# Layers 0, 2 and 3 of a diffusion transformer on one core: a block's outputs are turned back in the slot that turns a later block's maxima

## The reference, cut to what matters

```python
s = jnp.einsum('bqhd,bkhd->bhqk', q, k) * scale
a = jax.nn.softmax(s, axis=-1)
attn_out = jnp.einsum('bhqk,bkhd->bqhd', a, v).reshape(B, N, H)
x = x + gate_a[:, None] * (attn_out @ W_proj + b_proj)
```

## Time and profile before

| | |
|---|---|
| device time, three runs | 3444.96, 3454.8, 3452.23 us |
| the profiled execution: its own time | 3451.98 us |
| its span | 3450.2 us |
| mean granted TensorE clock | 0.95 of full |
| PE busy | 3162.4 us (92%) |
| DVE busy | 1824.0 us (53%) |
| ACT busy | 1467.0 us (43%) |
| POOL busy | 256.9 us (7%) |
| chain that ended last | PE 80%, DVE 10%, DMA 3%, ACT 3% |

### The profile page before, as it was taken

How to read it: one execution, slowest core, us unless ns; L and a number is a source line. 1 busy time by engine, 2 the same in 40 slices (tenths; PEclk the granted TensorE clock), 3 DMA queues, 4 the chain that set the end, 5 groups by cost and what they waited for, 6 DMA issues and landing times.

```text
span 3450.2 us, 52900 instructions
## 1 busy us (share of the span) xinstructions
PE 3162.4 (92%) x21156; PEld 1867.7 (54%) x21156; DVE 1824.0 (53%) x3812; ACT 1467.0 (43%) x2645; POOL 256.9 (7%) x278
## 2 busy tenths in 40 slices
PE   6899999999889999999389989999999999999987
PEld 3555665656566666666244445454454544554464
DVE  4876554563411322322278865757756577556433
ACT  0343535444322222221136645565455565565533
POOL 1100010001100000000100001001110101001010
PEclk9898999999898999999789999999999999999998
DMA  5200000002100000000321020001200000000000
GB/s 168 91 1 6 8 21 1 8 21 68 45 12 11 0 1 1 1 0 1 135 77 35 26 74 25 11 24 44 86 13 22 28 29 25 13 28 25 7 1 13
DMA packets 78713, 104.39 MB, mean 30 GB/s; under 512 B 18688, under 2 KB 52208, under 8 KB 78204
## 3 DMA queue, kind: packets, MB, share of 16 engines
q1 hardware_dynamic: 78468, 100.93, 8.9%
HBM read 72.05 MB, written 28.86 MB: 29 GB/s over the span
## 4 chain that ended last, share of the span: by engine, by line
PE 80%; DVE 10%; DMA 3%; ACT 3%; issue 2%; SPq 1%; POOL 1%; DVEq 0%; ACTq 0%; POOLq 0%
PE ps L978 73%; PE ps L1193 3%; DVE max_halves L1684 2%; DMA k_parts<-qk_parts 1%; PE ps L1320 1%; PE ps L1184 1%; DVE row_max_cross L1850 1%; DMA q_parts<-qk_parts 1%; PE ps L1172 1%; ACT big L2028 1%; ACT probs L2087 1%; DVE bn_stats L1720 1%; DMA q_blocks<-q_parts 1%; DVE xn_tok L1756 1%; SPq L879 1%
## 5 line engine op out<-in xcount | busy, mean ns | idle before, releaser
L2028 ACT ACTIVATE big<-ps 128x512 f32<-128x512 f32 x1280 | 693.7, 595 | 639.5 <-PE ps L978 638.6
L1684 DVE TENSOR_REDUCE max_halves<-ps 128x1 f32<-128x512 f32 x1024 | 650.4, 684 | 222.1 <-PE ps L978 219.4
L978 PE MATMUL ps<-k_groups,q_blocks 32*128 32x512 f32 x2048 | 451.6, 463 | 71.0 <-DVE qk_parts L1819 34.8
L978 PE MATMUL ps<-q_blocks,k_groups 32*128 32x512 f32 x2048 | 422.5, 466 | 3.3 <-DVE qk_parts L1819 2.0
L978 PE MATMUL ps<-big,probs 128*32 128x512 f32 (+2 forms) x3280 | 397.1, 531 | 5.0 <-ACT o_T L2003 3.8
L978 PE MATMUL ps<-weights_mlp,big 128*128 128x256 f32 (+1 forms) x1248 | 333.4, 419 | 2.5 <-ACT big L2099 2.5
L978 PEld LDWEIGHTS ps<-q_blocks,k_groups 32*128 32x128 f32 x2048 | 178.4, 185 | 286.1 <-issue 273.9
L978 PEld LDWEIGHTS ps<-weights_mlp,big 128*128 128x128 f32 x1248 | 233.7, 190 | 83.9 <-issue 58.0
L978 PEld LDWEIGHTS ps<-k_groups,q_blocks 32*128 32x128 f32 x2048 | 197.6, 189 | 120.9 <-DVE qk_parts L1819 39.0
L1726 DVE TENSOR_TENSOR x_tok<-ps,x_tok 128x512 f32<-128x512 f32 x112 | 77.3, 691 | 307.6 <-PE ps L978 307.4
L2087 ACT ACTIVATE probs<-ps 77x512 f32<-77x512 f32 x384 | 196.5, 592 | 96.8 <-PE ps L978 96.5
(11 more groups left out here) (233 smaller groups left out, 3913.6 us busy)
## 6 DMA issues: line engine op xcount, KB each, us to landing
q_blocks<-q_parts SPq DMA_DIRECT2D x64, 256.0 KB
q_parts<-qk_parts SPq DMA_DIRECT2D x48, 256.0 KB
k_parts<-qk_parts SPq DMA_DIRECT2D x32, 256.0 KB
k_groups<-k_parts SPq DMA_DIRECT2D x16, 512.0 KB
weights_mlp<-in_L_xcond_mlp_W SPq DMA_DIRECT2D x5, 1024.0 KB, 5.4
weights_mlp<-in_L_xcond_W_mlp SPq DMA_DIRECT2D x5, 1024.0 KB, 5.6
x_tok<-in_x SPq DMA_DIRECT2D x4, 1024.0 KB, 9.6
out_y<-x_tok SPq DMA_DIRECT2D x8, 512.0 KB, 2.9
```

The costliest lines, as they stand in the source:

```text
L978: return pe.matmul(out, lhsT, rhs, start=first, stop=last)
L1684: dve.tensor_reduce(NMP[:, e, j, qt, hf:hf + 1], PS[:, bank, :], AX.X, ALU.max, negate=True).then_inc(R.frees(key), 1)
L2028: act.activation(PB[:, score % 2, j, :], PS[:, R.bank(key), :], ACT.Exp, scale=SCALE).then_inc(R.frees(key), 1)
```

## The change

Only `slot_token` is touched. For a region that is not the masked version, the turning of block q no longer stands in the slot after its last product but in the next slot that turns maxima, at its end and just ahead of them. In layers 2 and 3 that is slot 8q+14 instead of 8q+9 (with the maxima of block q+2), in layer 0 slot 2q+4 instead of 2q+3 (with those of block q+3). The very last block's turning stays in the slot after its last product. In layers 2 and 3 the last but one has no maxima beside it any more and still moves by five slots. No instruction of the turning is added or dropped, but since the planner reads `tails` for its costs and conditions, all that it places between the slots from the first turning on is dealt anew.

```diff
             ahead = t + R.lead
-            tails = ((base + t - 2) // R.per,) if 2 <= t < count + 2 and (t - 1) % R.per == 0 else ()
             after = ahead - 1 if R.split else ahead
             nms = ((base + after) // R.per - 1,) if 0 < after <= count and after % R.per == 0 else ()
+            tails = ((base + count) // R.per - 1,) if t == count + 1 else ()
+            if not R.masked and after % R.per == 0 and R.per + 2 <= t <= count:
+                tails = ((base + t - 2) // R.per - 1,)
+            elif R.masked and 2 <= t <= count and (t - 1) % R.per == 0:
+                tails = ((base + t - 2) // R.per,)
```

## The result

The changed kernel takes 3470.28 us (median of 7, 3466.89 to 3488.34), the kernel before in the same comparison 3452.23 (median of 7). The two medians are 18 us apart. The ratio over all runs, which is not that of the medians, is 1.0073, 95% interval [1.0049, 1.0096]: slower, by 17 to 33 us. The forecast was 3454, a difference of 2.

The account below looks back on a forecast made before the run. PE was taken as the bound (busy 92% of the span), so only its waits counted. POOL's waits -7.5, layer 0's rest +5 and the rest of layers 2 and 3 +4.5 gave +2 on 3451.98: 3454 us, range 3438 to 3471.

Parts of the forecast that it names:

- the rest of layers 2 and 3: Stretch behind the last slot of layers 2 and 3: +4.5 us for nearly uncovered norm waits, bounds -8.5 to +8.5.
- the rests cost their full price: Rival, behind both regions' last slots: moved work finds no gaps, +10.5 and +8.5, POOL waits -4; 3467 us, chance 0.25.
- the slots gain more than the rests lose: Rival: POOL waits vanish (-12.7), rests add 2 each, ring wait goes in a third of blocks (-4.5); 3439 us, chance 0.17.
- The turning itself and its place in the ring: In the slots: turning costs the same anywhere, one bank wait replaces another; zero, bounds -13.5 to +13.5 us.
- The ring wait: 0.45 us in the slot after a turning, its fourth bank awaiting an exponential; forecast to recur at the new place.
- POOL's waits: PE's seven slot waits of the maxima's turning for POOL: 12.7 us become 5.2 in five, so -7.5.
- Other waits in the slots: PE's remaining 37 us of idle time in the slots of layers 2 and 3, dealt anew: zero, within 9 us.
- Layer 0: Its slots zero within 1 us; its rest +5 from uncovered waits (3.6) and clock (1.5), bounds -10 to +10.5.
- The clock behind joined transposes: Rival: the slot behind each joined pair of turnings runs at half clock, +174 us, 3626; chance 2%.
- The rule of the Trainium skill: Transposes don't count as PE clock activity like matmuls; rows of them could lower the clock, though the trace showed none.

Follow-up runs that it names:

- l2_only: Kernel before with the turning of the outputs moved in layers 2 and 3 only, layer 0 in its old order; 3470.66 us, ratio 1.0066.
- deal_only: Kernel before with other work of layers 2 and 3 dealt as if turnings came later, each turning left at its old slot; 3467.67 us, 1.0053.
- late_last: Kernel before with only the turning of the block before the last, in layers 2 and 3, moved to its new place; 3473.03 us, 1.0061.
- spread: Kernel before with the changed slot order in layers 2 and 3; their rest puts late-coming steps first, then follows the old order; 3448.39 us, 0.9999.
- place_only: Kernel before with its old dealing of other work; only afterwards turnings of blocks 0 to 5 of each batch put at the new place; 3445.84 us, 0.9994.
- l0_only: Kernel before with the turning moved in layer 0 only, layers 2 and 3 in their old order; 3450.47 us, 1.0010.
- last_early: Kernel before with all turnings moved except those of the last block and the one before it; 3447.95 us, 0.9995.
- spread_both: Kernel before with turnings moved in both regions, both rests putting late-coming steps first, then following the old order; 3452.01 us, 1.0012.

## Why the prediction was wrong

**The failed step is the rest of layers 2 and 3**, put at "+4.5 net" and "longer than 209 us by about 13". It is longer by 33 us in l2_only, deal_only and late_last, and by 40 in the changed kernel's profile. The 13 were made of 8.5 of moved work, 4.5 of uncovered waits and nothing for the clock. The first part of l2_only's rest is 30 us longer than before's (busy 41.1 to 62.3, idle 9.9 to 18.8): 8.5 of moved work, 8.9 more of idle time and 12.6 of clock, which fell from 1.00 to 0.81. The other 3 us are in the second part, where nothing was changed. Two terms were mis-sized then: the waits at half, and the clock at zero.

The waits for which I had allowed 4.5 did come, and as large as I had put them. PE's waits in that part, l2_only:

```profile
PE ps L985 <- ACT probs L2094: 6.1, 4, 1.7
PE ps L985 <- DVE row_max_cross L1857: 6.0, 4, 2.9
PE ps L985 <- issue: 2.3, 1, 2.3
PE ps L1200 <- DVE xn_tok L1763: 1.8, 1, 1.8
```

The last two are the new ones between projection and norm, 4.1 us. The others were longer waits of steps that had been there before: those for DVE's row maxima grew from 3.2 to 6.0 us (the maxima of both halves now follow each other), those for ACT's exponentials from 4.8 to 6.1. I had priced 1.5 us of clock in layer 0's rest from the earlier trace rows and none here, although that row (0.50 with PE busy 22 of 29 us) is four bare cross-attention steps; I had looked at which steps move into the rest, and not at what they take away from the steps that were there.

Even with the second half's work left between the steps, as in spread, the first part is 19 us longer than before's (69.9 against 51.0), not 13. That spread's whole rest is just 13 us longer in its profile (223.1 against 209.9) is luck: the second part happened to be 6 us shorter. By the first part and the shorter slots (-12, below) spread should still be some 7 us slower than before, and its time does not show it; that is open.

**The range.** 3470.28 lies within 3438 to 3471, by luck too. Its upper end was there for the scatter around a rival, and 16 us above the forecast are far more than the +2 that the sum gave.

**The rival "the rests cost their full price"** gave 3467, near the time, by another mechanism: it charged 8.5 for the moved work. Its own condition (PE's busy share in the rest stays at 82 to 85% while it grows by 12 us or more) nearly held, with 81% after 82, but a share of busy time hides a falling clock. The rival "the slots gain more than the rests lose" fell with the rests: it had 2 us for each, and they grew by 22 and 33.

**The turning itself and its place in the ring: zero.** Right. The ring wait did change its bank and stay. In the slot in which before had the turning of the earlier trace rows, PE's timeline of the changed kernel has it a little later, with ACT's exponential as the releaser:

```profile
1866.47 0.50 PE L982 MATMUL ps<-k_groups,q_blocks 32*128 32x512 f32 x1 [0.45 <-ACT big L2032]
...
1881.06 0.66 PE L1176 MATMUL ps<-ident,o_T 128*128 128x128 f32 x4
1881.55 0.60 PE L1188 MATMUL ps<-ident,row_max 128*128 128x128 f32 x4
1882.08 0.50 PE L982 MATMUL ps<-q_blocks,k_groups 32*128 32x512 f32 x2
```

The joined turnings take 1.02 us (1881.06 to 1882.08), 0.15 less than two apart. From the block's first product to the scores behind the next turned maxima it is 18.25 us (1863.83 to 1882.08), and 18.30 before (1860.50 to 1878.80). place_only puts the place of 24 of the 32 blocks in each region at -2 us [-7, +2] in all.

**POOL's waits: -7.5.** Five waits of about 1.0 us, 5.2 in sum, were forecast; five of at most 1.0 were there, 4.9 in sum: -7.8. PE's timeline has the wait ahead of block 26 as worked out:

```profile
2929.35 0.66 PE L1176 MATMUL ps<-ident,o_T 128*128 128x128 f32 x4
2931.05 0.66 PE L1188 MATMUL ps<-ident,row_max 128*128 128x128 f32 x4 [1.05 <-POOL row_max L2232]
```

**Other waits in the slots: 0 within 9.** The waits for exponentials grew by 5.5 us (25.2 to 30.7). In all, from the first scores of a present block in layers 2 and 3 (1763.99 before) to their last turning, the changed kernel's profile is 8 us shorter (1476.3 to 1468.0), where 7.5 + 8.5 = 16 were expected; in seven profiles with this order the stretch is 1453 to 1469, in three with the old one 1473 to 1476, so about 12 on average. That is 4 less than expected, and within the 9.

**Layer 0: +5.** The profile gives slots 17.1 us shorter and a rest 21.7 longer, +4.6; l0_only by itself is +3.5 [-1, +8] in time. Right within what can be told, though that is not much: kernels with the same order in layer 0 end it up to 10 us apart in their profiles.

**The clock behind joined transposes.** The stretch from 1880 to 1886, with such a pair in it, has a clock of 1.00 here too, and the slots as a whole 0.98, as before. The rule of the Trainium skill cited in the prediction (TensorE: Matmul & The Clock Gate, Part 4: PE-mode transpose) made no difference at this length. The clock mattered in the rest, where I had not looked for it; transposes stand among the slow steps there too (0.66 of a cross-attention step's 2.8 us at 2.4 GHz), and no run takes them out. The window around the pair:

```profile
1880.00:1886.00 6.00, 6.00 (x76) 3.00 (x76) 4.91 (x10) 4.12 (x8) 0.00 (x0) 1.00 0.01 3
```

Together: -12 in the slots and +33 in the rest make +21, and l2_only measured +21 (3470.66 against 3449.41; by its interval +17 to +29). That they meet to the microsecond is chance, since each term has a scatter of several us.

## What to carry to other kernels

When a change lets a greedy planner deal work anew, look at the end of its order first: a chain that starts a little later there meets its sister chain in the same phase, and the filler that each was for the other is gone. Price a bare chain of small steps with its waits and with TensorE's lower clock together; here the second was the larger. To avoid the loss of such a change, exempt the block that the last chain waits for (one of 32 made the whole loss); a gain was not left over here (last_early 0.9995). Compare busy time per instruction as well as idle time, since busy shares of 82 and 81% looked alike at 0.89 and at 0.80 of the clock. And split a stage at the point behind which the orders are the same: the part behind it shows how much one profile differs from the next by itself.

## What the runs showed of the hardware that I had not expected

- Where PE waited 1.3 us at a time between small steps, the clock stood at 1.2 GHz for most of the stretch: from 3272 to 3307 of the changed kernel PE was busy 26.7 of 35 us at a mean of 0.60. It isn't so each time: the four bare steps had 0.57 there (3285 to 3308) and 0.75 in l2_only.
- Eight matmuls of 256 bf16 columns (1.04 us) in each such wait brought 2.4 GHz back: at the end of the kernel the steps took 6.2 us without them in nine of ten profiles, and the last one 4.4 us with them in all four.
- The same order can keep or lose the clock from one execution to the next, and that alone is worth 11 us in 160: the second part of the rest took 153.2 us at 0.92 in spread (busy 124.6, idle 28.6) and 164.7 us at 0.83 in spread_both (busy 135.4, idle 29.3). The changed kernel's own seven runs lie at 3466.89 to 3470.28 (four, clock over the whole run 0.946 to 0.947) and at 3481.66 to 3488.34 (three, 0.940 to 0.942).
